# One transformer block: causal mask in the scores' contraction, 64-row maxima, three score banks

## The chip, the cores and the metric

The kernel runs on one core of one Trainium2 chip. The metric is the device time of one execution in microseconds (us); three runs of the kernel before gave 907.95, 909.5 and 906.62, median 907.95. The engines are TensorE (PE, its weight loads PEld), VectorE (DVE), ScalarE (ACT), GpSimd (POOL) and the queue engine SyncE (SP). PSUM has eight banks of 512 float32 columns.

## The reference, cut to what matters

Input x has 16 batches of 512 rows and 128 columns, float32. Each batch passes through feed-forward, attention and feed-forward again; nothing couples two batches.

```
x = x + 0.5 * ffn(layernorm(x))        # ffn: int4-quantised 128x128 weight, bias, low-rank term
x = x + attention(layernorm(x))        # 16 heads of 64, keys and values from a latent of 32 columns
x = x + 0.5 * ffn(layernorm(x))

# attention
q = x Wq;  lat = x Wkv_down;  k = lat Wk_up;  v = lat Wv_up
attn = q k^T / 8
attn = softmax(where(key <= query, attn, lowest float))     # causal
out = (attn v) Wout
```

## The kernel before, in words

**Data.** Keys and values come from a latent of 32 columns, so the key weights are folded into the queries. A query row is split into a high and a low part of reduced-precision float32 (`F32R`), stacked on 96 partitions, so that one product has three 32-row terms. Scores are made transposed: 128 keys on the partitions, queries along the columns. For a key tile j (0 to 3) of 128 keys only the queries from tile j on are computed: 512, 384, 256 or 128 columns per head. Heads go in four groups g of four.

**Two passes over the scores.** The softmax needs the largest score of each query. Pass one ("maxima", line 821) computes scores with 128 queries on the partitions and keys along the columns, masked by 26 further contraction rows that subtract a huge number where key > query. DVE reduces each bank to maxima (line 1088), PE transposes them (line 798), DVE negates them (line 1079), a DMA puts them into one more row of the stacked queries (`q_stack`). Pass two ("scores", line 752) contracts over 123 rows, so the negated maximum is added in the product, against plain key blocks, whose 26 mask rows are zero. ACT takes the exponential of each bank into `first_probs` (j = 0) or `later_probs` (j = 1 to 3, one buffer each) (line 601). POOL then zeroes the half of each diagonal 128x128 block where key > query (`affine_select`, line 524), one instruction per group and key tile: 16 per batch.

**Use of the probabilities.** "Weighing the latents" (`weigh_latents`, line 765) multiplies by the latent values into `y_bank`: eight matmul instructions per group and key tile. For the softmax's denominator POOL adds `later_probs` of j = 1 and 2 to `first_probs` (`add_probs`, line 491, two halves each); `weigh_ones` (line 784) sums over partitions: 32 instructions for `first_probs` of a group and 8 for its key tile 3, which POOL doesn't add. DVE inverts and spreads the result, POOL scales y (line 506), PE projects (`project_out`, line 901), then the second feed-forward (lines 915, 918).

**Stages.** Rounds t = -2 to 16. Round t attends batch t, makes the maxima of batch t+1 (`top`), prepares batch t+2 (`prep`: feed-forward, layernorm, queries, keys) and closes batch t-1 (`end`). Each engine has its own program. The order in a round is written out by hand: 16 steps (g, j), with tables that say at which step and slot a piece stands (`A_AT` for the maxima, `FRONT_AT`, `WEIGH`, `ADD_AT`, `TAIL_AT` and so on).

**PSUM.** Three banks (`ring`) for the 40 units of maxima and 2 transposes of a batch, two (`score0`, `score1`) for scores, one (`aux`) for preparation and closing, one for y, one for the denominators. A batch has 44 banks of scores (per group 4 + 4 + 2 + 1). In the last batch there are no maxima to make, so its scores use five banks, and DVE does the adds (line 1107).

**Waits around the change.** A score matmul waits until the exponential two banks earlier is done. A maxima unit waits until DVE has reduced the bank three units earlier. `weigh_latents` waits for POOL's select. An add waits for the select and for `weigh_latents` of j = 0. ACT may overwrite `later_probs` of j = 1 or 2 only when the adds of the group before are done. SP issues per round: placing the second half's maxima, latents, x back, next x, saved x, 12 query DMAs, first half's maxima, output, 3 key DMAs, 12 query DMAs, in this order, each behind its waits.

## Time and profile before

| | |
|---|---|
| runs, median (lowest to highest) | 907.95 us (906.62 to 909.5) |
| profiled execution, own time | 905.89 us |
| its span, first to last instruction | 904.2 us |
| mean granted TensorE clock | 0.983 of 2.4 GHz |
| busy PE / PEld / DVE / ACT / POOL | 93 / 64 / 73 / 61 / 81% of the span |

Busy time of PE counts a matmul from its start until its last column has left, so two matmuls in a row overlap and PE can be "busy" without streaming all the time. The distance between starts says how long one holds the engine. "Idle before" is time in which an engine had nothing running, put down to what ended it.

### The profile page before, as it was taken

The numbers are of one execution on the slowest core, as the hardware profiler recorded it, in microseconds if no ns is written. First come the engines' busy times: TensorE is split into PE (matmuls) and PEld (weight loads), VectorE is DVE, ScalarE is ACT, GpSimd is POOL, SyncE is SP. The second block draws the span as 40 slices with busy tenths as digits, with TensorE's granted clock in tenths as the row PEclk, the third lists the DMA queues.
The fourth block names the chain that finished last, engine by engine and source line by source line (L and its number), as shares of the span: only waits on it lengthen the run. The fifth ranks groups of instructions, "written<-read, shape, count | busy, mean of one in ns | idle before, by whom it ended". The sixth has DMA issues, their size and how long they took to land. (4 is left out here: it accounts for less than half of the span.)

```text
span 904.2 us, 21710 instructions
## 1 busy us (share of the span) xinstructions
PE 844.8 (93%) x7766; PEld 579.0 (64%) x7766; DVE 659.2 (73%) x1840; ACT 550.1 (61%) x1113; POOL 732.9 (81%) x834
## 2 busy tenths in 40 slices
PE   6688999999999999999999999999999999999886
PEld 4455666666576766667576766667676666757455
DVE  3597677678778677778868768877867767776645
ACT  4435666757666565757766665756766675656551
POOL 4304889998989989898998989898998999889732
PEclk9878999999999999999999999999999999999999
DMA  4445241524435151533535151443525152330000
GB/s 102 117 116 137 56 115 45 120 75 96 115 83 128 41 132 39 127 84 84 127 72 139 34 128 50 108 104 84 127 63 132 31 127 59 91 96 15 13 25 13
DMA packets 77547, 77.90 MB, mean 86 GB/s; under 512 B 9392, under 2 KB 51136, under 8 KB 77440
## 3 DMA queue, kind: packets, MB, share of 16 engines
q1 hardware_dynamic: 76640, 75.45, 34.5%
q8 instruction: 62, 1.02, 0.5%
q10 hardware_dynamic: 800, 1.07, 0.4%
q14 instruction: 45, 0.37, 0.1%
HBM read 9.90 MB, written 8.39 MB: 20 GB/s over the span
## 5 line engine op out<-in xcount | busy, mean ns | idle before, releaser
L491 POOL TENSOR_TENSOR first_probs<-first_probs,later_probs 128x768 f32<-128x768 f32 x240 | 371.4, 1556 | 23.0 <-PE bank L765 23.0
L601 ACT ACTIVATE later_probs<-bank 128x384 f32<-128x384 f32 (+1 forms) x448 | 231.0, 539 | 154.5 <-PE bank L752 154.2
L1088 DVE TENSOR_REDUCE maxima<-bank 128x1 f32<-128x512 f32 (+1 forms) x384 | 255.1, 682 | 62.0 <-PE bank L821 61.8
L752 PE MATMUL bank<-q_stack,keys 123*128 123x512 f32 (+1 forms) x704 | 280.5, 424 | 9.8 <-ACT first_probs L601 8.3
L821 PE MATMUL bank<-keys,q_stack 122*128 122x512 f32 (+3 forms) x1024 | 254.6, 337 | 10.1 <-DVE maxima L1088 2.5
L821 PEld LDWEIGHTS bank<-keys,q_stack 122*128 122x128 f32 x1024 | 181.3, 193 | 86.6 <-DVE block_max L1088 26.6
L601 ACT ACTIVATE first_probs<-bank 128x512 f32<-128x512 f32 x256 | 139.8, 594 | 98.8 <-PE bank L752 94.0
L1088 DVE TENSOR_REDUCE block_max<-bank 128x4 f32<-128x512 f32 x256 | 173.9, 679 | 32.8 <-PE bank L821 32.1
L752 PEld LDWEIGHTS bank<-q_stack,keys 123*128 123x128 f32 x704 | 127.9, 191 | 57.9 <-ACT first_probs L601 30.1
L524 POOL TENSOR_SCALAR_AFFINE_SELECT later_probs<-later_probs 128x512 f32<-128x512 f32 x192 | 124.0, 646 | 46.3 <-ACT later_probs L601 46.1
L765 PE MATMUL bank<-later_probs,lat 128*32 128x384 f32 (+2 forms) x1536 | 109.7, 388 | 0.7 <-POOL later_probs L524 0.7
L784 PEld LDWEIGHTS bank<-first_probs,group_ones 128*32 128x32 f32 x2048 | 58.7, 111 | 40.0 <-issue 35.5
L506 POOL TENSOR_TENSOR y_norm<-y_sb,y_norm 128x512 f32<-128x512 f32 x60 | 76.8, 1290 | 2.3 <-ACT first_probs L601 1.7
L784 PE MATMUL bank<-first_probs,group_ones 128*32 128x128 f32 x2048 | 68.6, 275 | 3.0 <-DVE first_probs L1107 3.0
L765 PE MATMUL bank<-first_probs,lat 128*32 128x512 f32 x512 | 69.1, 612 | 0.0
L765 PEld LDWEIGHTS bank<-later_probs,lat 128*32 128x32 f32 x1536 | 37.3, 109 | 43.5 <-issue 28.7
L901 PE MATMUL bank<-w_out,y_norm 128*128 128x128 f32 x512 | 60.3, 276 | 1.6 <-POOL y_norm L479 1.6
L901 PEld LDWEIGHTS bank<-w_out,y_norm 128*128 128x128 f32 x512 | 58.6, 192 | 3.6 <-POOL y_norm L479 2.1
L657 ACT ACTIVATE q_high<-bank 128x512 fp32r<-128x512 f32 x64 | 38.3, 599 | 34.0 <-PE bank L859 33.7
L1125 DVE STREAM_SHUFFLE y_norm<-den_inv 128x128 f32<-128x128 f32 x240 | 53.9, 302 | 0.0
L524 POOL TENSOR_SCALAR_AFFINE_SELECT first_probs<-first_probs 128x512 f32<-128x512 f32 x64 | 41.4, 646 | 15.3 <-ACT first_probs L601 15.3
L1200 DVE TENSOR_TENSOR q_low<-bank,q_high 128x512 fp32r<-128x512 f32 x64 | 43.6, 682 | 3.2 <-ACT q_high L657 3.2
(143 smaller groups left out, 898.6 us busy)
## 6 DMA issues: line engine op xcount, KB each, us to landing
q_stack<-q_high SPq DMA_DIRECT2D x256, 128.0 KB, 2.4
q_stack<-q_low SPq DMA_DIRECT2D x128, 128.0 KB, 2.5
out_dram<-x SPq DMA_DIRECT2D x32, 256.0 KB, 2.9
x_in<-in_L_attn_x_bld_dram SPq DMA_DIRECT2D x16, 256.0 KB, 3.3
x_back<-out_dram SPq DMA_DIRECT2D x16, 256.0 KB, 2.9
keys<-keys_staged SPq DMA_DIRECT2D x15, 192.0 KB, 2.5
keys<-keys_staged SPq DMA_DIRECT2D x30, 96.0 KB, 2.3
lat<-lat_staged SPq DMA_DIRECT2D x16, 64.0 KB, 1.9
```

Of the source, the lines that this page charges most:

```text
L491: nc.gpsimd.tensor_tensor(total, total, later_probs[j - 1][:, heads], ALU.add).then_inc(added, 1)
L506: nc.gpsimd.tensor_tensor(y_norm[:, g, :], y_sb[:, g, :], y_norm[:, g, :], ALU.mult).then_inc(y_normed, 1)
L524: nc.gpsimd.affine_select(out=diag, in_=diag, compare_op=ALU.is_ge, fill=0.0, base=0, pattern=[[0, HG], [1, n]], channel_multiplier=-1).th ...
L601: nc.scalar.activation(probs_of(s)[:, e:e + heads, 0:n], score_bank(t, u)[:, 0:heads * n].rearrange("p (e q) -> p e q", e=heads), ACT.Exp) ...
L752: nc.tensor.matmul(score_bank(t, u)[:, 0:heads * n], keys[par][:, PLAIN_BLOCK[j], :], q_stack[par][:, first:first + heads, j * P:L], start ...
L765: last = nc.tensor.matmul(y_bank[e * LD:(e + 1) * LD, j * P:L], lat[(par + off) % 2][:, j, :], probs_of(s)[:, e, 0:L - P * j], start=(j == ...
L784: last = nc.tensor.matmul(den_bank[e * LD:(e + 1) * LD, 0:P], group_ones[:, g * TT + i, :], probs_of(s)[:, e, (i - j) * P:(i - j + 1) * P] ...
L821: last = nc.tensor.matmul(bank[:, col:col + n], q_stack[1 - par][0:KC, half * HALF + h, j * P:(j + 1) * P], keys[1 - par][0:KC, blocks, :] ...
L901: last = nc.tensor.matmul(out_tile(t, i), y_norm[:, g, i * P:(i + 1) * P], w_out[:, g, :], start=(g == 0), stop=(g == G - 1))
L1088: nc.vector.tensor_reduce(out, seg, AX.X, ALU.max).then_inc(a_free, 1)
L1125: last = nc.vector.stream_shuffle(y_norm[:, g, i * P:(i + 1) * P], den_inv[:], [g * TT + i] * LD)
L1200: nc.vector.tensor_tensor(q_low[:, g, :], front_bank(t, 3 + g)[:], q_high[:, g, :].bitcast(F32), ALU.subtract).then_inc(f_free, 1)
```

## The change

The mask moves into the product of the scores too. It needs key blocks that carry mask rows also in pass two, so queries and keys are now laid out in strips of 64 (`HALF_TILE`): the stacked queries hold, per pair of heads, 8 strips of 2 x 64 queries; the keys lie in 34 strips of 64, with hidden, masked and plain copies. The mask takes 22 rows instead of 26, so that the contraction is 119 rows.

- **Scores.** Still 44 banks per batch, but a diagonal block (128 keys, 128 queries, 4 heads) has its own bank, made by two matmuls of 4 heads x 64 queries that write interleaved pieces of 64 columns; the rest of a key tile's columns are in other banks (384, 2 x 256 or 4 x 128 columns). 60 matmuls instead of 44, the same number of columns. All of a key tile's `affine_select` instructions are gone from POOL.
- **Maxima.** The stationary operand is 64 queries of two heads; the columns are the 64(w+1) keys they may see. 36 units of 512 columns and 2 transposes per batch instead of 40 and 2. After each half DVE does four small reductions and two copies instead of one and one.
- **Denominator.** POOL also adds key tile 3 (two more adds of 256 elements per group); `weigh_ones` does `first_probs` only.
- **Buffers.** `later_probs` is doubled. PSUM: three banks for scores, two for maxima. Early weights share memory with later buffers.
- **Keys.** Five DMAs instead of three, per batch.
- **Order.** Tables now count the 44 banks of a round; ranges of entries from 44 on belong to the next round. Maxima units are carried into the next round (five of them), the projection stands at bank 24, weighing and adds have a place of their own per group.

```diff
-QUINT = 5
-MASK_ROWS = -(-P // QUINT)
+TRIO = 3
+HALF_TILE = P // 2
+SUB = L // HALF_TILE
+MASK_ROWS = -(-HALF_TILE // TRIO)
-RING = 3
+RING = 2
-HALF_UNITS = ([unit for h in (0, 4, 2, 6) for unit in (
-    [(h, 3)], [(h, 2), (h, 0)], [(h + 1, 3)], [(h + 1, 2), (h + 1, 0)], [(h, 1), (h + 1, 1)])])
+HALF_UNITS = ([unit for p in (0, 2) for unit in (
+    [(p, 7)], [(p, 6), (p, 0)], [(p, 5), (p, 1)], [(p, 4), (p, 2)],
+    [(p + 1, 7)], [(p + 1, 6), (p + 1, 0)], [(p + 1, 5), (p + 1, 1)], [(p + 1, 4), (p + 1, 2)], [(p, 3), (p + 1, 3)])])
+PARTS_OF = [[None, (0, 1), (1, 1), (2, 1), (3, 1)], [None, (0, 2), (2, 2)], [None, (0, 4)], [None]]
+BANKS = [(g, j, part) for g in range(G) for j, parts in enumerate(PARTS_OF) for part in parts]
+MAX_AT = [
+    7, 7, 9, 10, 11, 11, 13, 15, 16, 18, 19, 20, 21, 21, 23, 23, 26, 27, 30, 32, 33, 34, 34, 36, 36, 39, 40, 41, 41,
+    42, 42, 43, 43, 44, 45, 46, 47, 50]
+FRONT_AT = [1, 4, 12, 16, 20, 28, 32, 40, 43]
+PROJECT_AT = [24, 24, 24, 24]
+TAIL_AT = [34, 37]
+WEIGH_AT = [[10, 10, 15, 15], [19, 19, 21, 21], [30, 30, 33, 33], [41, 51, 51, 51]]
+ONES_AT = [21, 33, 42, 51]
+ADD_AT = [[13, 13, 14, 15, 15, 19], [27, 27, 29, 29, 29, 35], [44, 44, 44, 46, 46, 46], [47, 47, 47, 52, 52, 53]]
-ADDED = [1, 2]
-DEN_PARTS = [3, 0]
+ADDED = [1, 2, 3]
...
-        later_probs = [sb(f"later_probs{j}", [P, HG, L - P * j]) for j in range(1, TT)]
+        later_probs = [[sb(f"later_probs{j}_{i}", [P, HG, L - P * j]) for j in range(1, TT)] for i in range(2)]
-        ring, (aux, score0, score1, y_bank, den_bank) = banks[:RING], banks[RING:]
+        ring, (third, aux, score0, score1, y_bank, den_bank) = banks[:RING], banks[RING:]
+        score_banks = [score0, score1, third]
...
         def place_keys(eng, par):
 
-            for to, of in ((slice(1, 5), slice(0, 4)), (slice(5, 7), slice(0, 2)), (slice(0, 8, 7), slice(2, 4))):
-                eng.dma_start(keys[par][0:KS, to, :].bitcast(F32), staged[:, of, :]).then_inc(keys_landed, DMA)
+            for to, step, of, of_step, at_once, count in PLACES:
+                eng.dma_start(every(keys[par][0:KS].bitcast(F32), to, step, at_once, count),
+                              every(staged, of, of_step, at_once, count)).then_inc(keys_landed, DMA)
...
-                        wait_batch_alone(pool, exp_done, t, 0, SCORES, score_unit(s, HG - 1) + 1)
-                        diag = probs_of(s)[:, :, 0:n]
-                        nc.gpsimd.affine_select(out=diag, in_=diag, compare_op=ALU.is_ge, fill=0.0, base=0,
-                                                pattern=[[0, HG], [1, n]], channel_multiplier=-1).then_inc(p_ready, 1)
...
+                def score(u):
+
+                    g, j, part = BANKS[u]
+                    n, bank = L - P * j, score_bank(t, u)
...
-                        wait_batch(pe, exp_done, t, 0, SCORES, u - 1)
-                    nc.tensor.matmul(score_bank(t, u)[:, 0:heads * n], keys[par][:, PLAIN_BLOCK[j], :],
-                                     q_stack[par][:, first:first + heads, j * P:L], start=True, stop=True).then_inc(s_full, 1)
+                        wait_batch(pe, exp_done, t, 0, SCORES, u - len(score_banks) + 1)
+                    pair, of = g // 2 * PAIRS, g % 2
+                    if part is None:
+                        for half in range(2):
+                            w = 2 * j + half
+                            out = bank[:].rearrange("p (e q) -> p e q", e=HG)[:, :, half * HALF_TILE:(half + 1) * HALF_TILE]
+                            last = nc.tensor.matmul(out, strips(par, KM, OWN[w]), q_stack[par][:, pair:pair + HG, w, of, :],
+                                                    start=True, stop=True)
+                    else:
+                        e, heads = part
+                        last = nc.tensor.matmul(bank[:, 0:heads * (n - P)], strips(par, KM, LATER[j]),
+                                                q_stack[par][:, pair + e:pair + e + heads, 2 * (j + 1):SUB, of, :],
+                                                start=True, stop=True)
+                    last.then_inc(s_full, 1)
...
-                    wait_batch(pe, p_ready, t, off, STEPS, s + 1)
+                    wait_batch(pe, exp_done, t, off, SCORES, scores_by(g * TT + j))
...
+                        for of, first, end in ((0, 0, 7), (1, 0, 3), (2, 0, 5), (2, 5, 8)):
+                            w = (6, 5, 4)[of] if first == 0 else 2
+                            nc.vector.tensor_reduce(maxima[:, half, :, w], strip_max[:, half, of, :, first:end], AX.X, ALU.max)
+                        nc.vector.tensor_copy(maxima[:, half, :, 0], strip_max[:, half, 0, :, 7])
+                        nc.vector.tensor_copy(maxima[:, half, :, 1], strip_max[:, half, 1, :, 3]).then_inc(max_made, 1)
```

## Rows read from the trace of the kernel before

**Rows 1.** Page: busy us (share of the span) and instructions; tenths in 40 slices.
```profile
span 904.2 us, 21710 instructions
PE 844.8 (93%) x7766; PEld 579.0 (64%) x7766; DVE 659.2 (73%) x1840; ACT 550.1 (61%) x1113; POOL 732.9 (81%) x834
...
POOL 4304889998989989898998989898998999889732
```

**Rows 2.** PE in order of time, each round's projection: start, us, instruction.
```profile
145.95 3.75 PE L901 MATMUL bank<-w_out,y_norm 128*128 128x128 f32 x32
...
762.79 3.75 PE L901 MATMUL bank<-w_out,y_norm 128*128 128x128 f32 x32
...
812.70 3.73 PE L901 MATMUL bank<-w_out,y_norm 128*128 128x128 f32 x32
857.68 3.84 PE L901 MATMUL bank<-w_out,y_norm 128*128 128x128 f32 x32
```

**Rows 3.** Busy time in four stretches: columns as in the first line.
```profile
core 0: us, PE busy (x) PEld busy (x) DVE busy (x) ACT busy (x) POOL busy (x), PEclk, DMA share, GB/s
41.00:75.00 34.00, 26.60 (x95) 18.28 (x96) 30.66 (x66) 13.39 (x19) 3.40 (x8) 0.79 0.54 129
403.00:454.40 51.40, 49.96 (x479) 34.56 (x479) 39.37 (x113) 33.29 (x69) 46.63 (x51) 1.00 0.38 93
812.70:857.70 45.00, 41.54 (x419) 26.78 (x417) 28.89 (x80) 26.06 (x53) 37.83 (x39) 0.96 0.05 14
```

**Rows 4.** Waits in the round 403.0 to 454.4: us in total, times, longest.
```profile
POOL later_probs L524 <- ACT later_probs L601: 2.2, 5, 1.0
DVE x L1163 <- POOL xb L541: 2.1, 1, 2.1
...
PEld bank L752 <- ACT first_probs L601: 1.6, 4, 0.9
PEld bank L821 <- DVE block_max L1088: 1.6, 4, 0.6
...
POOL first_probs L491 <- PE bank L765: 1.4, 2, 1.0
```

**Rows 5.** POOL by line and form: busy us, mean ns; idle before.
```profile
L491 POOL TENSOR_TENSOR first_probs<-first_probs,later_probs 128x768 f32<-128x768 f32 x120 | 219.2, 1827 | 23.0 <-PE bank L765 23.0
L491 POOL TENSOR_TENSOR first_probs<-first_probs,later_probs 128x512 f32<-128x512 f32 x120 | 152.1, 1285 | 0.0
L524 POOL TENSOR_SCALAR_AFFINE_SELECT later_probs<-later_probs 128x512 f32<-128x512 f32 x192 | 124.0, 646 | 46.3 <-ACT later_probs L601 46.1
...
L524 POOL TENSOR_SCALAR_AFFINE_SELECT first_probs<-first_probs 128x512 f32<-128x512 f32 x64 | 41.4, 646 | 15.3 <-ACT first_probs L601 15.3
```

**Rows 6.** PE in order of time, parts of one round.
```profile
420.21 0.41 PE L821 MATMUL bank<-keys,q_stack 122*128 122x256 f32 x2
420.46 0.41 PE L752 MATMUL bank<-q_stack,keys 123*128 123x512 f32 x1
420.70 1.06 PE L918 MATMUL bank<-w_ffn,xn_t 128*128 128x128 f32 x8
...
422.71 0.40 PE L784 MATMUL bank<-later_probs,group_ones 128*32 128x128 f32 x8
423.05 0.45 PE L752 MATMUL bank<-q_stack,keys 123*128 123x384 f32 x1
...
439.44 0.92 PE L821 MATMUL bank<-keys,q_stack 122*128 122x512 f32 x5
440.19 0.39 PE L752 MATMUL bank<-q_stack,keys 123*128 123x512 f32 x1
```

**Rows 7.** DVE by line and form: busy us, mean ns; idle before.
```profile
L1088 DVE TENSOR_REDUCE maxima<-bank 128x1 f32<-128x512 f32 x256 | 174.3, 681 | 29.0 <-PE bank L821 28.8
...
L1094 DVE COPY maxima<-block_max 128x8 f32<-128x8 f32 x32 | 10.5, 328 | 0.0
...
L1093 DVE TENSOR_REDUCE maxima<-block_max 128x8 f32<-128x24 f32 x32 | 5.7, 180 | 1.1
```

More of the change, by code:

```diff
@@ new lines @@
+FRONT_AT = [1, 4, 12, 16, 20, 28, 32, 40, 43]
[3 more added lines that the diff above has]
+ONES_AT = [21, 33, 42, 51]
+LAST_WEIGH_AT = [[9, 15, 15, 15], [20, 22, 22, 23], [33, 33, 33, 33], [40, 55, 55, 61]]
+LAST_ONES_AT = [23, 31, 61, 64]
+assert all(a <= b for at in (MAX_AT, FIRST_MAX_AT) for a, b in zip(at, [*at[1:], MAX_AT[0] + SCORES]))
+MASK_AT = [5, 6, 22, 24]
+FRONT_ACT_AT = [2, 3, 13, 18, 22, 29, 33, 39, 43]
@@ L220, in score_bank @@
+        mask_k = first_probs[1][KS:KC, 0, 0:HALF_TILE]
+        ring, (third, aux, score0, score1, y_bank, den_bank) = banks[:RING], banks[RING:]
+        spare = [*ring, third]
+        score_banks = [score0, score1, third]
+        wide_scores = [*ring, *(score_banks[((B - 1) * SCORES + WIDE_FROM + i) % 3] for i in range(3))]
         def score_bank(t, u):
@@ L683, in one_round @@
+                    for i in range(TT):
+                        if end and u == TAIL_NORM_AT[i]:
+                            tail_normalise(i)
+                    for off, there in ((-1, end), (0, attend)):
+                        for g in range(G):
+                            if there and u - SCORES * off == READ_AT[g]:
+                                read_y(off, g)
                 if is_first(t):
@@ L711, in query_products @@
                         rows = slice(odd * HD, (odd + 1) * HD)
-                        last = nc.tensor.matmul(ring[odd][:, j * LD:(j + 1) * LD], wq_t[rows, j, :], wk_t[rows, j, :],
+                        last = nc.tensor.matmul(spare[odd][:, j * LD:(j + 1) * LD], wq_t[rows, j, :], wk_t[rows, j, :],
                                                 start=True, stop=True)
@@ L838, in front_unit @@
                         wait_batch(pe, f_free, t, 2, F_UNITS, u)
[L839 removed]
                     if end:
+                        turns = sum(at <= FRONT_AT[u] for at in (PROJECT_AT[-1], *TAIL_AT))
                         wait_batch(pe, t_free, t, -1, T_UNITS, turns)
@@ L868, in tail_waits @@
                     if prep:
-                        turns = sum(s < TAIL_AT[u] for s in front_at)
+                        turns = sum(at < (PROJECT_AT[0], *TAIL_AT)[u] for at in FRONT_AT)
                         wait_batch(pe, f_free, t, 2, F_UNITS, turns)
@@ new lines, in max_unit @@
+                    if w == 7:
+                        out, strip = maxima[:, half, p, w:w + 1], L
+                    elif w == 3:
+                        out, strip = maxima[:, half, p:p + 2, w], (w + 1) * HALF_TILE
+                    else:
+                        strip = P if w == 5 else HALF_TILE
+                        out = strip_max[:, half, 6 - w, p, 0:L // strip]
+                    nc.vector.tensor_reduce(out, bank[:].rearrange("q (b k) -> q b k", k=strip), AX.X,
+                                            ALU.max).then_inc(a_free, 1)
@@ new lines, in last_add @@
+                def last_add(off, g, j, part, turn):
+                    if g == 0 and turn == 0:
+                        wait_batch(dve, den_done, t, off, G, 0)
+                    wait_batch(dve, pv_done, t, off, STEPS, g * TT + 1)
+                    wait_batch(dve, exp_done, t, off, SCORES, scores_by(g * TT + j))
+                    wait_batch(dve, added, t, off, G * GROUP_ADDS, g * GROUP_ADDS + turn - PARTS + 1)
+                    heads = slice(part * HG // PARTS, (part + 1) * HG // PARTS)
+                    total = first_probs[g % 2][:, heads, j * P:L]
+                    nc.vector.tensor_tensor(total, total, probs_of(g, j)[:, heads],
+                                            ALU.add).then_inc(added, 1)
```

727 lines of the change are left out of this document (322 added, 405 removed).

## The prediction

> **What bounds the kernel now.** I read the page's busy shares first. PE is busy 93% of the span and POOL 81%, and POOL's row of slices is at 8 or 9 tenths from the fifth slice until the kernel drains [rows 1]. Two engines are candidates, so the next view is the length of a round. The projection comes once per round: 145.95 us, and 762.79 us twelve rounds later, so a steady round lasts 616.84/12 = 51.40 us; the next two last 49.91 and 44.98 us [rows 2]. In one such round POOL is busy 46.63 us of 51.4, PE 49.96, DVE 39.37, ACT 33.29, at the full granted clock of 1.00, that is 2.4 GHz [rows 3]. PE's busy time flatters it: the weight-load row beside it is 34.56 us, and a 512-column score matmul that is busy 0.39 to 0.41 us lets the next start 0.24 us later (420.46 to 420.70 in the order of time; here the pair of 256 columns before it, 420.21 to 420.46, holds PE 0.25 us) [rows 3, 6]. POOL's busy time doesn't overlap in that way: it has only 51.4 - 46.63 = 4.77 us left per round, and 2.2 + 1.4 = 3.6 us of these it waits for ACT's exponentials or for PE's weighing [rows 4], waits that exist because the select stands in a chain exponential, select, weighing, add. So POOL sets the round, with PE close behind through that chain. DVE and ACT have 12 and 18 us to spare.
>
> **The change part by part, per round of one batch.**
>
> *Selects removed (POOL).* 16 x 0.646 = 10.3 us of POOL [rows 5]. With them go the wait of 2.2 us for ACT in front of them, and a hop of 0.65 us between exponential and weighing.
>
> *Third added block (POOL).* Two adds of 256 elements per group, 8 per round. The trace has adds of 768 elements at 1.827 us and 512 at 1.285 us [rows 5]: 2.12 ns an element and 0.20 us fixed, so 256 take 0.74 us; 8 x 0.74 = 5.9 us. Bounds: no less than the select of 512 elements, 0.646, would give 5.2 us; no more than a 512-element add 10.3 us. The line through two points is close, I take 5.9.
>
> POOL's balance: 46.63 - 10.3 + 5.9 = 42.2 us. If its 4.77 us of other time stay, the round is 47.0 us.
>
> *Sums of ones (PE).* Eight instructions for key tile 3 per group go: 423.05 - 422.71 = 0.34 us each time [rows 6], four times, 1.3 us of PE. The sum for a group now needs six adds done instead of four and the wait falls on PE; behind it in PE's queue stand scores. The adds stand 8 banks or so between weighing of key tile 0 (bank 10) and the sum (bank 21) for group 0, where 2 x (1.83 + 1.29 + 0.74) = 7.7 us are needed and eleven banks of a 47 us round are 11.8 us: covered, by 4 us.
>
> *Maxima (PE and DVE).* 36 units instead of 40. A burst of five matmuls that make three units holds PE 440.19 - 439.44 = 0.75 us, 0.25 us a unit [rows 6]: 1.0 us less on PE. DVE loses four reductions of 0.68 us, 2.7 us, and gains per half three small reductions at 0.18 and a copy at 0.33 [rows 7], 2 x 0.87 = 1.7 us: -1.0 us on DVE, which isn't the bound.
>
> *Scores (PE and ACT).* The same 44 banks and columns; ACT's 44 exponentials keep their sizes (28 of 512, 16 of 384), so ACT changes by nothing. 16 banks are now made by two matmuls of 256 columns. The nearest row is the pair of 256-column maxima matmuls, 0.25 us for both against 0.24 for one of 512 [rows 6]: 16 x 0.01, nothing. That pair reads keys in separate pieces too, but writes PSUM in one run; no row shows a matmul that writes pieces of 64 columns apart. Bounds: nothing, and double time, 16 x 0.25 = 4 us. I take nothing. Weights are loaded 16 times more, beside running matmuls: PEld has 17 us free in a round [rows 3].
>
> The Trainium skill says otherwise here: its page "SBUF — State Buffer", section "Door 1: The DMA port swizzle", holds that any non-contiguous PSUM access pattern significantly slows down matmuls. No row of this trace tests it; it is a rival below.
>
> *Three score banks, two for maxima.* PE waits 1.6 us per round for ACT before a score (line 752) and 1.6 us for DVE before a maxima unit [rows 4]. The third bank takes most of the first away, the missing one adds to the second. I cost them against each other at nothing; bounds -1.6 us and, if each of 36 units waits for the reduction one place nearer (0.6 us apart), far more: that is a rival.
>
> *Doubled `later_probs`, keys, order.* ACT waits for no adds in rows 4, so the doubling gives nothing by itself. Two more key DMAs per round stand in SP's queue ahead of 12 query DMAs; keys are staged at bank 42 and first read at bank 7 of the next round, 9 banks or 9 us later: covered. SP's second-half maxima now wait until bank 6; the x that comes back is read at bank 26: covered. The wait of DVE for POOL's `xb`, 2.1 us [rows 4], goes as the add stands earlier in a shorter queue; DVE has room, so nothing.
>
> **Sum.** Steady rounds: 51.4 - 47.0 = 4.4 us. Scores run from 75 us on, where the stretch of maxima alone ends, and 762.79 - 75 = 688 us are 13.4 such rounds: 13.4 x 4.4 = 59.0 us. In the rounds of 49.9 and 45.0 us POOL has more room (37.83 busy of 45.0 [rows 3]), so they save only PE's share, 1.3 + 1.0 = 2.3 us each, 4.6 together. In the last batch DVE does the adds, eight more of them, at 0.3 to 0.7 us each by its 512-element reduction of 0.68 [rows 7], and the hop over the select goes 16 times; I set these against each other. The stretch 41 to 75 us, where maxima alone are made and DVE is busy 30.66 of 34 us [rows 3], is DVE's: four units at 0.6 us less, 1.7 us more, -0.8 us. POOL's longer memsets before 41 us run where POOL is 3 to 4 tenths busy [rows 1]. Together 64 us. The profiled execution took 905.89 us with a span of 904.2; less 64 that is 842. The median of the runs stands 2.1 us above it: 844 us.
>
> **Rivals.**
>
> 1. *The waits go too.* Without the select the chain exponential, weighing, add is shorter, and POOL's 3.6 us of waits vanish: round 43.4 us. For it: these waits are all on lines that the select was part of. Against it: PE. Taking away 2.3 us of work leaves it 49.1 us if none of its own waits goes, and it must lose 5.7 us of them. Time: 908 - 13.4 x 8.0 - 5 = 796 us; half way 820. Chance 0.18.
>
> 2. *PE was the bound after all.* Then only its 2.3 us count: round 49.1 us, 908 - 13.4 x 2.3 - 5 = 872 us. For it: PE is busy 49.96 of 51.4. The skill ("Trainium Kernel Development and Optimization", section "Performance Expectations") calls matmul busy time a bad metric, and points to the weight loads; here these are 34.56 of 51.4 us, which speaks against this rival. Chance 0.14.
>
> 3. *The other side: two banks for maxima.* With three banks a burst of three units goes through while DVE reduces at 0.6 us a piece; with two, the third waits in PE's queue, in order, with scores and weighings behind it. PE's round is 49.1 us if its waits stay as they are, so that the change turns slower once each of the 36 units waits 2.3/36 = 0.064 us longer than now. At 0.15 us each, the round is 54.5 us, the time 908 + 13.4 x 3.1 - 5 = 945 us. For it: PE already waits for DVE on that line [rows 4]. Against it: `MAX_AT` sets at most two units at one bank, and DVE has 12 us of slack. Chance 0.10.
>
> 4. *Writes in pieces are slow.* At double time 4 us more on PE, 53.1 us if PE's other waits stay and 51.5 if the third bank gives 1.6 back, so 904 to 926 us. That is the page's rule worked as this kernel would feel it; nothing in rows 6 speaks for it. Chance 0.06.
>
> **How the numbers follow.** Forecast (round of 46 to 48.5 us) 0.52, rivals 0.18, 0.14, 0.10, 0.06. The likeliest case gives 844 us, own range 828 to 862. The range for 8 in 10 reaches half into rival 1 and through rival 2: 812 to 882 us; left out are the rest of rival 1 and rivals 3 and 4. Slower by more than 0.3% (the least that a measurement of this kernel tells from no change, 2.7 us): most of rivals 3 and 4, 0.10. Within 0.3%: 0.03. Faster: 0.87.
>
> **What would show it.** Right: POOL busy near 42 us per round, a projection every 47 us, no line of selects; adds of 256 elements at 0.74 us; the pair of 256-column score matmuls 0.25 us from start to start of the next; line of ones 1.3 us shorter per round. Wrong: a round above 49 us with POOL well under 42/49 busy (rival 2), PE waiting for DVE's reductions over 4 us per round (rival 3), the pairs above 0.4 us (rival 4), or POOL and PE both waiting for each other at places where a weighing stands before its exponentials.

## Result and the profile after

The changed kernel takes 850.51 us (median of four runs, 847.87 to 861.11) against 908.04 us for the kernel before beside it: ratio 0.9357, 95% interval [0.932, 0.9393]. 844 us was predicted, with 812 to 882 as the range. The slowest of the four ran in a slower state of the chip (mean granted clock 0.954, the others 0.965 to 0.969), and the ratio goes by the other three, whose mean is 849.6 us. The profiled execution took 847.87 us, with a span of 846.1 us, 58.1 us less than the span of before.

The page after: busy us, share of the span, instructions; tenths in 40 slices. These answer to [rows 1].
```profile
span 846.1 us, 21032 instructions
...
PE 785.8 (93%) x7518; PEld 591.7 (70%) x7518; DVE 662.7 (78%) x1912; ACT 540.5 (64%) x1113; POOL 661.6 (78%) x694
...
POOL 4501787989799998979799997989899998879612
PEclk9855999999999999999999999999999999999999
```
POOL has 71 us less busy time, PE 59, DVE 3.5 more. PEclk dips to 5 in the third and fourth slices.

PE in order of time, the first instructions of four projections of the kernel after (answering to [rows 2]).
```profile
148.21 0.50 PE L937 MATMUL bank<-w_out,y_norm 128*128 128x128 f32 x3
...
719.11 0.50 PE L937 MATMUL bank<-w_out,y_norm 128*128 128x128 f32 x3
...
764.14 0.51 PE L937 MATMUL bank<-w_out,y_norm 128*128 128x128 f32 x3
...
806.06 0.63 PE L937 MATMUL bank<-w_out,y_norm 128*128 128x128 f32 x2
```
L937 is the projection (`project_out`) of this kernel. Twelve steady rounds take 719.11 - 148.21 = 570.90 us, 47.58 each; before they took 51.40. They come in two lengths, 47.25 and 48.03. Where the 58.1 us are:

| stretch | before | after | difference | forecast |
|---|---|---|---|---|
| start to first projection | 145.95 | 148.21 | +2.3 | -7.0 (1.4 rounds of 4.4, and -0.8) |
| 12 steady rounds | 616.84 | 570.90 | -45.9 (3.83 a round) | -52.8 (4.4 a round) |
| next two rounds | 94.89 | 86.95 | -7.9 | -4.6 |
| from there to the end | 46.5 | 40.0 | -6.5 | 0 |

Busy time of the kernel after in a long and a short round, and where the clock dips (answering to [rows 3]).
```profile
core 0: us, PE busy (x) PEld busy (x) DVE busy (x) ACT busy (x) POOL busy (x), PEclk, DMA share, GB/s
386.74:434.77 48.03, 45.71 (x463) 34.85 (x462) 39.94 (x117) 32.65 (x70) 42.39 (x43) 1.00 0.43 104
434.77:482.01 47.24, 45.62 (x462) 34.83 (x462) 39.16 (x117) 32.62 (x70) 42.34 (x43) 1.00 0.44 105
50.00:80.00 30.00, 26.78 (x76) 20.24 (x77) 23.07 (x50) 11.55 (x18) 3.00 (x6) 0.50 0.35 84
```
POOL is at 42.4 us as forecast, with 5 us to spare. PE has 2.3 us to spare in the long round. The view of waits gives nearly all of this to one line: PE in the round 386.74 to 434.77, in us, times, longest (answering to [rows 4]).
```profile
PE bank L841 <- DVE maxima L1097: 2.2, 1, 2.2
```
L841 is the transpose of the maxima, and L1096 and L1097 are the two copies on DVE ahead of it, where the kernel before has one. DVE, POOL and PE of the kernel after around one such wait, in order of time.
```profile
412.65 0.41 DVE L1095 TENSOR_REDUCE maxima<-strip_max 128x4 f32<-128x28 f32 x4
412.98 2.37 DVE L1096 COPY maxima<-strip_max 128x4 f32<-128x4 f32 x1
415.26 0.16 DVE L1097 COPY maxima<-strip_max 128x4 f32<-128x4 f32 x1
...
412.67 2.66 POOL L545 TENSOR_TENSOR first_probs<-first_probs,later_probs 128x512 f32<-128x512 f32 x3
...
412.96 0.39 PE L801 MATMUL bank<-q_stack,keys 119*128 119x512 f32 x1
415.57 0.27 PE L841 MATMUL bank<-identity,maxima 128*32 128x128 f32 x1 [2.21 <-DVE maxima L1097]
```
A copy of four elements per partition takes 2.37 us. It starts 0.31 us after POOL began three adds in a row, and ends, at 415.35, as these end, at 415.33. The next copy takes 0.16. In the short rounds the first copy lasts 1.00 us, until the first of the three adds ends, and the second 0.77, until the second ends. Everything behind the transpose in PE's queue stands for 2.21 us. The sums of a whole run show that it is no single case: DVE and POOL by line and form, busy us, mean ns (answering to [rows 7] and [rows 5]).
```profile
L1096 DVE COPY maxima<-strip_max 128x4 f32<-128x4 f32 x32 | 24.1, 754 | 0.0
...
L1097 DVE COPY maxima<-strip_max 128x4 f32<-128x4 f32 x32 | 10.1, 314 | 0.0
...
L545 POOL TENSOR_TENSOR first_probs<-first_probs,later_probs 128x768 f32<-128x768 f32 x120 | 217.0, 1830 | 1.9 <-PE bank L814 1.8
L545 POOL TENSOR_TENSOR first_probs<-first_probs,later_probs 128x512 f32<-128x512 f32 x120 | 152.5, 1289 | 0.0
L545 POOL TENSOR_TENSOR first_probs<-first_probs,later_probs 128x256 f32<-128x256 f32 x120 | 87.1, 738 | 0.0
```
The view of the tile `maxima` adds that L1096 took 159 ns at least, 165 in the median and 2383 at most, and the view of waits over the whole run that PE stood 25.5 us in 15 waits for L1097, 1.7 us a round. The Trainium skill's "SBUF — State Buffer", section "Who interferes with whom", has VectorE's copies, where their operands allow a mode with two ports, and GpSimd share a pair of ports, held by whoever came first for a whole instruction, while `tensor_reduce` stays out of it. The trace agrees: where the copy is long, its end falls on the end of an add, and e1 below tests the reductions. It goes further: this copy waited through three adds, not one.

Where PE's round went: the distances from each PE row to the start of the next, summed by the stage that the first row belongs to, over ten steady rounds and divided by ten. Waits are in it (the 2.2 us above are under scores, whose row is the one before). e5 and e1 are experiments below.

| us per round | before | after | e5 | e1 |
|---|---|---|---|---|
| scores | 14.07 | 13.46 | 13.93 | 12.07 |
| maxima | 11.93 | 10.27 | 12.16 | 10.22 |
| weighing | 9.36 | 9.37 | 9.38 | 9.37 |
| preparation | 5.93 | 5.67 | 7.02 | 5.66 |
| ones | 5.27 | 3.97 | 3.97 | 3.97 |
| projection, closing, transposes | 4.84 | 4.83 | 4.82 | 4.81 |
| sum | 51.4 | 47.6 | 51.3 | 46.1 |

PE of the kernel after in order of time, around a score bank made by a pair of 256-column matmuls that write pieces (answering to [rows 6]).
```profile
440.35 0.40 PE L801 MATMUL bank<-q_stack,keys 119*128 119x512 f32 x1
440.58 0.40 PE L797 MATMUL bank<-q_stack,keys 119*128 119x256 f32 x2
440.82 0.40 PE L857 MATMUL bank<-keys,q_stack 118*128 118x512 f32 x1
```
The pair holds PE for 0.24 us, the single matmul of 512 columns for 0.23.

### The profile page after: what moved, and what is told of

The parts are those of the page before. It is cut to its first block and busy times, and to the rows that moved or that the text cites. A ratio compares the mean times of both kernels' runs of the same rounds, so it can differ in the third digit from the quotient of the medians.

```text
span 846.1 us, 21032 instructions
## 1 busy us (share of the span) xinstructions
PE 785.8 (93%) x7518; PEld 591.7 (70%) x7518; DVE 662.7 (78%) x1912; ACT 540.5 (64%) x1113; POOL 661.6 (78%) x694
## 5 line engine op out<-in xcount | busy, mean ns | idle before, releaser
L545 POOL TENSOR_TENSOR first_probs<-first_probs,later_probs 128x768 f32<-128x768 f32 x360 | 450.6, 1286 | 1.9 <-PE bank L814 1.8
L1089 DVE TENSOR_REDUCE strip_max<-bank 128x8 f32<-128x512 f32 (+1 forms) x384 | 254.8, 684 | 32.4 <-PE bank L857 29.4
L641 ACT ACTIVATE later_probs<-bank 128x512 f32<-128x512 f32 x384 | 216.2, 598 | 63.5 <-PE bank L801 41.2
L857 PE MATMUL bank<-keys,q_stack 118*128 118x512 f32 (+7 forms) x1024 | 230.4, 317 | 5.9 <-DVE strip_max L1089 3.0
L857 PEld LDWEIGHTS bank<-keys,q_stack 118*128 118x128 f32 x1024 | 179.3, 198 | 29.0 <-DVE strip_max L1089 10.8
L641 ACT ACTIVATE first_probs<-bank 128x384 f32<-128x384 f32 (+1 forms) x320 | 146.2, 516 | 69.0 <-PE bank L801 51.4
L801 PE MATMUL bank<-q_stack,keys 119*128 119x384 f32 (+1 forms) x448 | 171.8, 409 | 0.0
L1089 DVE TENSOR_REDUCE maxima<-bank 128x1 f32<-128x512 f32 (+1 forms) x192 | 129.6, 682 | 27.5 <-PE bank L857 27.4
L797 PE MATMUL bank<-q_stack,keys 119*128 119x256 f32 x512 | 116.1, 309 | 0.0
L801 PEld LDWEIGHTS bank<-q_stack,keys 119*128 119x128 f32 x448 | 80.9, 190 | 38.5 <-ACT later_probs L641 29.5
L797 PEld LDWEIGHTS bank<-q_stack,keys 119*128 119x128 f32 x512 | 83.8, 189 | 32.5 <-issue 18.3
L814 PEld LDWEIGHTS bank<-later_probs,lat 128*32 128x32 f32 x1536 | 42.7, 110 | 58.1 <-ACT later_probs L641 20.8
L937 PE MATMUL bank<-w_out,y_norm 128*128 128x128 f32 x512 | 60.8, 277 | 1.5 <-POOL y_norm L533 1.5
L937 PEld LDWEIGHTS bank<-w_out,y_norm 128*128 128x128 f32 x512 | 59.9, 194 | 2.1 <-POOL y_norm L533 2.1
```

The source lines that it names most:

```text
L545: nc.gpsimd.tensor_tensor(total, total, probs_of(g, j)[:, heads], ALU.add).then_inc(added, 1)
L641: nc.scalar.activation(out, score_bank(t, u)[:, 0:heads * cols].rearrange("p (e q) -> p e q", e=heads), ACT.Exp).then_inc(exp_done, 1)
L797: last = nc.tensor.matmul(out, strips(par, KM, OWN[w]), q_stack[par][:, pair:pair + HG, w, of, :], start=True, stop=True)
L801: last = nc.tensor.matmul(bank[:, 0:heads * (n - P)], strips(par, KM, LATER[j]), q_stack[par][:, pair + e:pair + e + heads, 2 * (j + 1):SU ...
L814: last = nc.tensor.matmul(y_bank[e * LD:(e + 1) * LD, j * P:L], lat[(par + off) % 2][:, j, :], probs_of(g, j)[:, e, 0:L - P * j], start=(j ...
L857: last = nc.tensor.matmul(bank[:, col:col + n], queries, strips((par + off) % 2, KC, SEEN[w]), start=True, stop=True)
```

## Experiments

Two questions were open: whether POOL's work set the round of before, as the prediction had it, and what the parts of the change are worth alone. Ratios are to the kernel before, run beside each.

**e1_reduce_for_copy.** The kernel after, with the two copies as reductions over one element:
```diff
-nc.vector.tensor_copy(maxima[:, half, :, 0], strip_max[:, half, 0, :, 7])
-nc.vector.tensor_copy(maxima[:, half, :, 1], strip_max[:, half, 1, :, 3]).then_inc(max_made, 1)
+nc.vector.tensor_reduce(maxima[:, half, :, 0], strip_max[:, half, 0, :, 7:8], AX.X, ALU.max)
+nc.vector.tensor_reduce(maxima[:, half, :, 1], strip_max[:, half, 1, :, 3:4], AX.X, ALU.max).then_inc(max_made, 1)
```


> The changed kernel with the two small DVE copies of a half's maxima (128x4 each) written as reductions over an axis of length one; the values are the same. Theory A: the copy of 2.37 us at 412.98 us of the changed kernel's trace lasts until POOL's adds end at 415.33, so DVE and POOL share something that this copy needs and a reduction does not. Then both operations take about 0.16 us, PE's idle time before the transpose (25.5 us in 15 waits) falls to under 8 us, a steady round goes from 47.6 to about 45.7 us, and the time from 850.5 to about 828 us. Theory B: the copy waits for something else (its writes behind the reductions before it, or the maxima themselves being late), and any operation in its place waits as long: 850 us within 2. Theory C: the stall goes but POOL (42.4 us busy of 47.6) or the order then holds the round: 840 to 848 us.

Measured: 824.98 us, ratio 0.9092 [0.9075, 0.9109], as theory A had it. DVE's two lines, and busy time in one round.
```profile
L1097 DVE TENSOR_REDUCE maxima<-strip_max 128x4 f32<-128x4 f32 x32 | 4.8, 151 | 0.0
L1096 DVE TENSOR_REDUCE maxima<-strip_max 128x4 f32<-128x4 f32 x32 | 4.8, 151 | 0.0
```
```profile
core 0: us, PE busy (x) PEld busy (x) DVE busy (x) ACT busy (x) POOL busy (x), PEclk, DMA share, GB/s
329.01:374.81 45.80, 45.67 (x463) 34.83 (x463) 37.70 (x117) 32.64 (x70) 42.42 (x43) 1.00 0.45 108
```
The round is 45.80 us and PE has 0.13 of it free. 47.25 = 45.80 + 1.45 and 48.03 = 45.80 + 2.23: the two lengths of round after are this one plus the shorter or the longer stall. The stall cost some 24.5 us, by the mean times (849.6 and 825.1) as by the profiled spans (846.1 and 821.7). Three of the twelve rounds still last 46.6 to 47.2 us. What ends PE's wait there, and SP ahead of it:
```profile
448.68 0.70 PE L857 MATMUL bank<-keys,q_stack 118*128 118x512 f32 x3 [0.97 <-DMA keys<-keys_staged]
```
```profile
442.20 3.34 SPq L376 DMA_DIRECT2D keys<-keys_staged  x5
```
Five key transfers take SP 3.34 us to issue, 0.67 each. In the kernel after PE waits for no keys in these rounds, as it comes late.

**e2_before_small_select.** The kernel before, whose selects treat one head of four (the mask of the others is left out):
```diff
-diag = probs_of(s)[:, :, 0:n]
+diag = probs_of(s)[:, 0:1, 0:n]
...
```


> The kernel before with each of POOL's 16 selects per round done on one head of four (128 elements of 512); three heads of four keep their unmasked probabilities. All waits and all of PE's, DVE's and ACT's work stay. It takes 16 x (0.65 - 0.29) = 5.7 us of POOL per round away. Theory 'POOL set the round': the round falls from 51.4 by most of that until PE holds it at about 49.1 plus the 2.3 us of PE work that this kernel still has, less what PE waited for POOL and ACT: 47 to 49.5 us a round, 850 to 883 us in all. Rival 'PE was the bound': the round stays above 50.7 us, 899 to 908 us.

Measured: 907.88 us, ratio 1.0014 [0.9995, 1.0033]. One round of it:
```profile
403.00:454.73 51.73, 50.24 (x481) 34.50 (x477) 39.91 (x114) 33.34 (x70) 41.22 (x51) 1.00 0.38 92
```
POOL has 5.4 us less to do than in [rows 3], and the round is 0.3 us longer. The 0.3 us are the copy again, which now falls beside POOL's adds. DVE's copy and the transpose behind it, in before and then in e2:
```profile
432.20 0.49 DVE L1094 COPY maxima<-block_max 128x8 f32<-128x8 f32 x1
433.09 0.27 PE L798 MATMUL bank<-identity,maxima 128*32 128x128 f32 x1
```
```profile
435.72 1.05 DVE L1094 COPY maxima<-block_max 128x8 f32<-128x8 f32 x1
436.92 0.27 PE L798 MATMUL bank<-identity,maxima 128*32 128x128 f32 x1
```
In before the copy ends 0.40 us ahead of the transpose, in e2 0.15, and PE's row ahead of the transpose holds it 0.31 us longer. Less these 0.31 the round is 51.4 us, as before. POOL did not set the round of before.

**e3_pool_more.** The kernel after, with eight selects of 512 elements on a scratch tile added per round:
```diff
+if attend and u % 5 == 2 and u < 40:
+    pool.wait_ge(scratch_made, 1 + 8 * t + u // 5)
+    nc.gpsimd.affine_select(out=scratch[:], in_=scratch[:], ...).then_inc(scratch_made, 1)
...
```


> The changed kernel with eight more selects of 512 elements per round on POOL, on a scratch tile that nothing else reads (8 x 0.65 = 5.2 us per round more on POOL, 42.4 to 47.6 us busy of a round that was 47.6). Theory 'POOL still sets the round': all 5.2 us appear, round 52.5 us, time about 920 us. Theory 'PE with its waits sets it now': POOL had about 5 us free, so the round grows by 0 to 2.5 us, 850 to 885 us.

Measured: 913.38 us, ratio 1.0066 [1.0034, 1.0098]. Two rounds of it, and PE's longest sum of waits over the run:
```profile
200.66:251.35 50.69, 46.41 (x461) 34.80 (x462) 39.98 (x117) 32.61 (x70) 47.18 (x51) 1.00 0.41 98
407.78:461.18 53.40, 50.46 (x461) 38.63 (x462) 38.92 (x117) 33.03 (x70) 47.14 (x51) 0.90 0.39 93
```
```profile
PE bank L837 <- POOL first_probs L547: 31.9, 17, 2.4
```
POOL's added work is 4.8 us by its busy time (42.39 to 47.18). In the two rounds that ran wholly at the full granted clock the round is 50.7 us, 3.1 more than after, with PE waiting 2.4 us for POOL's adds at the sums of ones. From 355.40 to 725.09 us the rounds last 52.8 on average at a granted clock of 0.90 to 0.93: PE waits the same 2.4 us, and behind that wait, from 430 to 440 us in the second round shown, the granted clock is 0.54 and 0.50 (1.2 GHz). So some 2 us of the 5.2 more a round are the clock and not POOL's work as such. The ten runs go with it: 907 us at a mean clock of 0.95, 920 at 0.916. It lies between the two theories, nearer to the first. The kernel after with its selects kept was not run; with 10.3 us more on POOL than 42.4 it would pass 47.6 us. The changed order needs most of them gone, though shortening them in the kernel before gives nothing.

**e5_two_scores_three_maxima.** The kernel after with the banks of before:
```diff
-RING = 2
+RING = 3
-score_banks = [score0, score1, third]
+score_banks = [score0, score1]
-return score_banks[(t * SCORES + u) % 3]
+return score_banks[(t * SCORES + u) % 2]
...
```


> The changed kernel with PSUM as before: two banks for scores, three for maxima, everything else and the order kept. My prediction set the two banks against each other at nothing: 848 to 854 us. Rival 'the third score bank is needed by this order': PE waits for ACT before scores at most banks; 0.3 us at half of the 44 score banks gives 6.6 us a round and 930 us. Rival 'the missing maxima bank costs': this kernel is faster, 840 us or less.

Measured: 895.69 us, ratio 0.9862 [0.9846, 0.9879]. One round, and what PE's weight loads wait for in it:
```profile
403.45:454.74 51.29, 47.74 (x462) 34.96 (x462) 39.16 (x117) 33.36 (x70) 42.40 (x43) 1.00 0.41 97
```
```profile
PEld bank L797 <- ACT later_probs L641: 2.7, 4, 1.6
PEld bank L801 <- ACT later_probs L641: 2.3, 4, 0.8
...
PEld bank L801 <- ACT first_probs L641: 1.7, 4, 0.7
```
POOL and PE have the work of the kernel after, and the round is as long as before. The three waits are 6.7 us, against 1.6 for `first_probs` in [rows 4] and 0.6 more for `later_probs`. No theory had the price: 3.7 us a round, where the rival said 6.6. The order written for three score banks waits for exponentials when it has two. Its span is 10.3 us shorter than before, mostly outside the steady rounds: the next two last 92.0 us (94.9 before), and from the 15th projection to that of the last batch it takes 23.6 us (before 30.6, after 24.2).

**e6_before_three_scores.** The opposite: the kernel before, its order and work unchanged, with three banks for scores and two for maxima.
```diff
-RING = 3
+RING = 2
-return (score0, score1)[u % 2]
+return score_banks[(t * SCORES + u) % 3]
-wait_batch(pe, exp_done, t, 0, SCORES, u - 1)
+wait_batch(pe, exp_done, t, 0, SCORES, u - 2)
...
```


> The kernel before with its PSUM banks split as in the change: three for scores, two for maxima, everything else and the order kept. Known by now: taking 5.4 us of POOL's work per round off the kernel before (51.73 us a round) gave nothing, and two score banks in the changed kernel gave 51.3 us a round. Theory 'two locks': the two score banks hold PE at about 51 us a round and POOL's 46.6 us of work with its waits hold it there as well, so this one alone gives at most 1 us a round: 893 to 908 us. Rival 'the score bank alone': the round falls to 48.5 or less, below 870 us. Rival 'order': the order written for three maxima banks stalls with two, slower than 912 us.

Measured: 982.77 us, ratio 1.0848 [1.0823, 1.0873]; rounds of 55.9 and 57.1 us. PE's weight loads, waits over the run:
```profile
PEld bank L823 <- DVE block_max L1090: 92.1, 117, 1.5
PEld bank L823 <- DVE maxima L1090: 69.7, 142, 1.6
```
In before the same two stood at 26.6 and 16.8 us over the run. This is rival 3 of the prediction as it was written, with its price of some 5 us a round, in the old order: bursts of three units meet two banks. The bank moved to scores is worth -46 us in the new order (ratios 0.9862 and 0.9357) and +77 in the old one (1.0848).

**e9_before_three_scores_small_select.** e6 with the selects of e2, to see whether banks and selects help only together:
```diff
-diag = probs_of(s)[:, :, 0:n]
+diag = probs_of(s)[:, 0:1, 0:n]
```


> The kernel before with three score banks, two for maxima, and POOL's selects on one head of four (three heads of four keep their unmasked probabilities). Theory 'two locks': with both open the round falls although neither alone did it: PE has 2.3 us more work than the changed kernel, so 48 to 50 us a round, 855 to 888 us. Rival 'the order and the shorter chain of the change are what counts': 895 us or more.

Measured: 992.05 us, ratio 1.0951 [1.0929, 1.0973]; the wait for `block_max` is 91.4 us as in e6. It's the order that goes with the banks, not the selects. It is 9 us slower than e6 with less work on POOL, rounds of 56.5 and 57.7 us. Most of this is the copy once more: its longest is 1.23 us (e6 0.67), and the wait of the transpose for it 6.8 us in 15 waits (e6 0.3).

**e10_reduce_for_copy_pool_less.** e1, with the adds of key tile 3 cut to 16 of 128 columns (the denominators lack the rest):
```diff
+end_at = j * P + 16 if j == 3 else L
...
```


> The version with reductions in place of the copies (824.98 us, round 45.80 us) with POOL's third adds cut to 16 of 128 columns; the denominators lack the rest of key tile 3. It takes 8 x 0.47 = 3.8 us of POOL's 42.4 us per round. Theory 'PE is the bound at 45.8 us' (busy 45.67 of 45.80): 825 us within 3. Rival 'POOL at 42.4 busy plus its waits is the bound': up to 3.8 us a round less, 775 to 800 us.

Measured: 821.22 us, ratio 0.907 [0.9044, 0.9096], overlapping e1's interval. One round:
```profile
329.00:374.60 45.60, 45.60 (x464) 34.86 (x463) 37.68 (x116) 32.65 (x70) 38.66 (x43) 1.00 0.45 109
```
3.8 us less on POOL shorten the round by 0.2, and PE is busy all of it. So POOL does not set this round; e12 below adds PE work to it.

**e8_reduce_for_copy_pe_busy.** e1, with two extra matmuls of 128 columns per maxima unit in the first round that makes maxima, for the dip of PEclk:
```diff
+if t == -1:
+    for _ in range(EXTRA):
+        nc.tensor.matmul(score0[:, 0:P], identity[:], ones[:], start=True, stop=True)
```


> The version with reductions in place of the copies, and two more 128x128 float32 matmuls into an unused score bank before every maxima unit in the round that makes maxima alone (round -1). In the changed kernel PE's granted clock is 0.50 from 40 to 80 us, in the kernel before 0.65 to 1.00, and the first projection comes at 148.2 instead of 145.9 us. Theory 'the slow clock costs the start': with more matmul work the clock is granted fully in this stretch, and the start is 2 to 6 us shorter: 819 to 823 us. Rival 'DVE paces this stretch': the clock may rise but the added work eats it: 825 us within 2; or the clock stays at 0.50 and the time grows by up to 8 us.

Measured: 820.76 us, ratio 0.9053 [0.903, 0.9075], the fastest version that leaves no work out. The stretch 50 to 80 us:
```profile
50.00:80.00 30.00, 29.30 (x198) 25.30 (x198) 25.67 (x53) 12.52 (x20) 2.93 (x5) 1.00 0.38 92
```
The granted clock is 1.00 there (2.4 GHz), where it was 0.50 (1.2 GHz) after and in e1, and the first projection starts at 141.40 us, in e1 at 144.35. The intervals of e1 and e8 touch at 0.9075, so it is the profiles that show the 3 us and not the medians. They agree in five runs: with the extra matmuls the first projection starts at 141.40 and 142.37 us (e11), without them at 144.35, 146.48 (e10) and 144.73 (e12).

**e11_keys_from_two_queues.** e8, with two of the five key transfers issued by ACT:
```diff
-place_keys(sp, par)
+place_keys(sp, par, PLACES[0:3])
+place_keys(act, par, PLACES[3:])
```


> The version with reductions in place of the copies and the extra matmuls in round -1 (820.76 us), with two of the five key DMAs of each round issued by ACT after its last exponential of the round instead of by SP. In the trace of the version with reductions, SP issues the five in 3.34 us (0.67 each), the last lands just before the first maxima unit wants it, and in every third or fourth round PE waits 0.8 to 1.4 us for the keys. Theory 'issue time': the keys land 1.3 us sooner, the long rounds (46.8 us) become 45.8 us, four or five of them: 815 to 818 us. Rival: ACT's two issues (0.6 us each) and its wait delay the exponentials of the next round, and the time is 821 us or more.

Measured: 827.2 us, ratio 0.9112 [0.9096, 0.9128], worse than e8. Only one of its twelve rounds is longer than the others (46.8), but those are 46.4, not 45.8: PE now waits 0.36 us, in the round from 374.42, for an exponential (6.0 us in 14 waits over the run). That it stands behind ACT's issues fits the order of ACT's program and was not tested. The longer rounds cost e8 0.7 to 1.1 us four times in twelve; this costs 0.6 every time.

**e12_third_block_by_ones.** e1, with key tile 3 back in PE's sums, as before, and off POOL:
```diff
-ADDED = [1, 2, 3]
+ADDED = [1, 2]
+for e in range(HG):
+    last = nc.tensor.matmul(den_bank[e * LD:(e + 1) * LD, 0:P], group_ones[:, g * TT + 3, :],
+                            probs_of(g, 3)[:, e, 0:P], start=False, stop=(g == G - 1))
...
```


> The version with reductions in place of the copies (824.98 us, PE busy 45.67 of 45.80 us a round), with the third block undone alone: POOL adds key tiles 1 and 2 only (5.9 us a round less), and PE sums key tile 3 with eight more matmul instructions per group. Theory 'PE is the bound': its 4 x 0.24 to 0.33 = 1.0 to 1.3 us a round appear in full, 837 to 844 us, and POOL's relief gives nothing back. Rival 'POOL and PE share the bound': 825 us or less.

Measured: 833.8 us, ratio 0.9181 [0.9161, 0.9201], 8 us over e1. The last seven of its twelve rounds last 46.45 us, +0.65 on e1; the first five 47.2 to 47.8, with 5.0 us of waits for keys in the five together. Behind the 32 sums of `first_probs` the eight hold PE 0.33 us, and the 32 then hold 0.87 to 0.90 instead of 0.98 to 1.01: 0.22 net, 0.9 in a round. That the block is on POOL is worth this. In such a round PE is busy 46.43 of 46.43 us and POOL 36.94. 5.5 us less on POOL bought nothing, and 0.9 us more on PE cost 0.65: PE sets the round of e1.

**e14_before_fewer_ones.** The kernel before, with two instead of eight sums for key tile 3 in three groups (parts of the denominators left out):
```diff
-for e in range(HG):
+for e in range(1 if j == 3 and g else HG):
```


> The kernel before with PE's sum of key tile 3 into the denominators done for one head of four in three of the four groups (2 instructions instead of 8; those denominators lack it). Everything else, POOL's 46.6 us a round included, stays. The eight hold PE 0.33 us, so 3 x 0.2 to 0.25 = 0.6 to 0.75 us of PE's work per round go. Theory 'PE was the bound of the kernel before' (its round didn't move when 5.4 us of POOL's work went): 8 to 10 us less, 896 to 900 us. Rival 'the order of scores and exponentials with two banks held it, PE's own work didn't': 905 us or more, the gap turning into waits before scores.

Measured: 907.8 us, ratio 0.9996 [0.9981, 1.001]. It doesn't tell the theories apart: two such instructions hold PE 0.31 us (412.88 to 413.19), eight hold 0.33 (449.75 to 450.08), so that the edit removed 0.06 us a round.

**e15_before_no_third_ones.** The same, with all eight left out in three groups:
```diff
+if j == 3 and g:
+    pe.sem_inc(den_done, 1)
+    return
```


> The kernel before, with PE's sum over key tile 3 left out wholly in groups 1 to 3 (the denominators of these groups lack that key tile; group 0 keeps its eight sums). In the trace of before, eight such sums hold PE for 0.33 us, so this takes 3 x 0.33 = 1.0 us from PE in a round and nothing from any other engine. Theory A (PE's own work, with what it waits for between its stages, was what set the round of before): the round falls by about 1.0 us, to 50.4, and 13.4 rounds give 13 us: 893 to 897 us. Theory B (the loop of score banks and exponentials with two banks holds the round, and PE's sums lie in its slack): the round stays at 51.2 or more, 905 us or more. Theory C (POOL sets the round, as the prediction had it): 907 to 908 us, as before, since nothing of POOL's is changed.

Measured: 901.08 us, ratio 0.9926 [0.9898, 0.9954]. One round:
```profile
402.95:453.95 51.00, 49.43 (x456) 33.94 (x456) 39.37 (x113) 33.26 (x69) 46.67 (x51) 1.00 0.38 93
```
It lies between what theories A and B gave. The round is 0.4 us shorter, with POOL's work unchanged at 46.67. The distances in the round from 401.95 us, laid beside those in the round from 402.93 of before, say where the 1.0 us went. The 16 weighings ahead of each of the removed sums held PE 0.67 us and now hold 0.79, three times, so the sums cost 0.22 net each (as in e12) and 0.66 in the round. 0.22 of these come back in one longer wait, of PE's weight load for DVE's `q_low`; in before and then in e15:
```profile
412.12 0.19 PEld L857 LDWEIGHTS bank<-x_high,query_low 128*128 128x128 f32 x1 [0.32 <-DVE q_low L1200]
```
```profile
411.17 0.19 PEld L860 LDWEIGHTS bank<-x_high,query_low 128*128 128x128 f32 x1 [0.54 <-DVE q_low L1203]
```
Two thirds of the work that left PE came out of the round, and in e2 none of what left POOL. So PE's own work lay on the path that set the round of before, with waits for DVE and ACT in it.

## Why the prediction was right, and where its reasons were wrong

The time fell where it was forecast (850.5 for 844), in part by luck. The step that carries the sum, "So POOL sets the round", failed, and two errors of opposite sign hid it: PE lost more time than the forecast asked of it, and a stall that no term had took some of it back.

- **POOL's balance.** Each size was right: adds of 256 elements 738 ns (forecast 0.74 us), POOL at 42.4 us per round (42.2). What failed is "If its 4.77 us of other time stay": that time was slack. In e1 it shrinks to 45.80 - 42.42 = 3.4 us, and in before 5.4 us of work could go for nothing (e2). In e3, where POOL does hold PE up, 50.69 - 47.18 = 3.5 us are left, so that POOL's 42.4 us would allow about 45.9 by themselves (an estimate): in e1 the two engines' bounds lie close together. A busy share of 91% with 3.6 us of waits inside is no proof of a bound. e3 shows what one looks like: at the full clock 4.8 us of added work give 3.1 us of round, and another engine waits 2.4 us for this one.
- **PE's floor.** The prediction put PE at 49.1 us "if none of its own waits goes", under a forecast of 47.0 us: the forecast needed 2.1 us of PE's waits to go, and no term of it said which. They went, and more: without the stall the round is 45.8 us, 5.6 less than before. By the table above, where e1's longer rounds are in the mean of 46.1, 5.3 us are gone: 1.3 of the ones (as forecast), 1.7 of the maxima (1.0 forecast), 2.0 of the scores (nothing forecast) and 0.3 of the preparation.
- **The banks.** "I cost them against each other at nothing", bounds -1.6 us and a loss. In the new order the exchange is worth 51.29 - 47.58 = 3.7 us a round, nearly all of the steady gain of 3.8. Both pay for the copies, but not alike: over the run PE stands 11.1 us behind L1097 in e5 and 25.5 after, 0.7 and 1.7 us a round, so that without the copies it would be about 4.7 (an estimate). In the old order it costs 4.5 to 5.8. Neither the bank nor the order can be priced alone. Rival 3 was sound as a mechanism, and what speaks against it in the prediction (at most two units at one bank of the order) fits what decided; no run changes this alone.
- **The copies.** The one more was counted at 0.33 us of DVE, where DVE has room. Their mean is 0.75 and 0.31, but one of them stands on PE's path: +1.45 or +2.2 us a round. The mean of 328 ns in [rows 7] for a copy of fewer elements than the reductions of 180 ns beside it was the sign. Its spread in the trace of before is 162 ns at least, 174 in the median, 996 at most.
- **Rivals.** Rival 1 (waits go too, 796 us, half way 820) is nearest to e1's 825 us in number, but not in mechanism: POOL kept 3.4 us of other time, where the rival left it 1.2. The prediction's objection to it, that PE must lose 5.7 us of waits, holds in part: PE lost 5.6 - 2.3 = 3.3. Rival 2 had PE as the bound, which holds for e1 (e10, e12), but not its price, since PE's waits went. Rival 4, and with it the rule of the Trainium skill that it worked out ("SBUF — State Buffer", "Door 1: The DMA port swizzle"), isn't seen: the pair holds PE 0.24 us, within 0.01 of the forecast.
- **Doubled `later_probs`, keys, order.** "Covered" for the two more key transfers was true only behind the stall; without it PE waits 0.97 us for keys in the round shown, and three of e1's twelve rounds are 0.8 to 1.4 us longer. The doubling was not tried alone.
- **Ends.** The start, forecast at -7.0 us, came out at +2.3: the granted clock of 50 to 80 us fell from 0.78 to 0.50, and e8 gives 3 us of this back. One stall of 2 us, at 125 us, stands in it too; the rest stays open, and runs with the same start scatter by 2 us (144.35 in e1, 146.48 in e10). The drain, forecast at nothing, gave 6.5 us. From the 15th to the 16th projection PE is busy 25.97 of 30.61 us before and 23.14 of 24.22 after; there PE's loads waited 2.5 us for POOL's selects, and none does after. The granted clock differs as well, 0.94 before and 0.97 after. At a clock of 1.00 the stretch lasts 28.96 us in e14, which leaves the selects alone, 28.05 in e2 with short selects, and 23.60 in e5, with the new work and the old banks. So of the 7.0 us between before and e5 up to 1.7 are the clock, 0.9 the shorter selects, and 4.4 order and work together, not told apart.

What stays open: no run has the new order with the old work, or the mask in the product or the maxima in strips of 64 alone, so that the gain of the steady rounds is not divided between work and order, but for key tile 3 (e12).

## What to carry to other kernels

Before an engine is called the bound, ask what the forecast needs of the next one: a round of 47.0 us needed 2.1 us of PE's waits to vanish, and naming them would have pointed to the banks and the order. A buffer count and the order written for it are one edit, to be priced and tested together (-46 us in one order, +77 in the other). Look at the longest duration of a small instruction, not at its mean only, and at what stands behind it: here two lines were worth some 24.5 us. And before a run with added work is read as a bound, look at the granted clock of its rounds: in e3 the clock was some 2 of 5.2 us.

## What the runs showed of the hardware

- A DVE copy of 128x4 float32 between SBUF tiles took 159 ns at least and up to 2383 ns beside POOL's `tensor_tensor`, ending with POOL's third add in a row; a `tensor_reduce` over one element of the same data took 148 to 155 ns (e1). Where POOL's instructions were moved or shortened, the stall came and went: one of the two copies of 128x8 in a round took 0.49 us in most rounds of before, 1.05 in e2.
- From 50 to 80 us the granted clock was 0.50 (1.2 GHz) in the kernel after, where PE was busy 26.78 us, and 1.00 (2.4 GHz) in e8, with 29.30; in the kernel before it was 0.78 on average, with 24.48. The kernel before was busy for less and was granted more, which I had not expected.
- Behind PE's wait of 2.4 us in a round of e3 the granted clock was 0.54 and 0.50 from 430 to 440 us, and 0.94 from 440 to 445; with PE busy 3.57 of 5 us ahead of it (425 to 430).
- Two sums into 32 columns held PE for 0.31 us and eight for 0.33 (e14), so that the number of them is hardly in the price. Eight between weighings and a maxima matmul cost 0.22 net, as the weighings hold PE 0.12 us longer when the maxima matmul follows them directly (e15).
- Two matmuls of 256 columns, writing pieces of 64 columns, held PE no longer than one of 512 that writes one run (0.24 and 0.23 us).
